# A selective-scan layer with feed-forward: a prologue of its own on six PSUM banks, one table set for Exp and Ln, and twelve units added by VectorE

## What is computed

```python
xz = einsum('bld,ed->ble', hidden, in_proj_w); x, z = xz[..., :1024], xz[..., 1024:]
x = silu(causal_conv4(x, conv_w) + conv_b)
x_dbl = einsum('bld,ed->ble', x, x_proj_w)         # 64 for dt, 16 for B, 16 for C
dt = softplus(einsum(x_dbl[..., :64], dt_proj_w) + dt_proj_b)
A = -exp(A_log)
h = exp(dt * A) * h + dt * x * B                   # per channel and state, over 4096 tokens
y = (sum over n of h * C + x * D) * silu(z)
x1 = layernorm(hidden + einsum(y, out_proj_w))
out = layernorm(x1 + relu(x1 @ Wq1.T + b1) @ Wq2.T + b2)   # Wq: W quantised to -1, 0, 1
```

## Time and profile before

| what | value |
|---|---|
| median of 3 runs | 4861.68 us (4856.44 to 4863.53) |
| profiled execution | 4863.47 us, its span 4861.4 us |
| first scan starts | 91.85 us |
| last scan ends | 3829.8 us |
| busy over the span | PE 92%, DVE 81%, ACT 74%, POOL 66% |

### The profile page before, as it was taken

One profiled execution on the slowest core, in us unless ns is written; L12 is line 12 of the kernel. 1 busy time (PEld: TensorE's weight loads), 2 busy tenths in 40 slices (PEclk: granted clock), 3 DMA queues, 4 the chain that ended last, 5 costly groups with the idle time before them and its releaser, 6 DMA issues.

```text
span 4861.4 us, 85854 instructions
## 1 busy us (share of the span) xinstructions
PE 4458.8 (92%) x23618; PEld 3170.0 (65%) x23618; DVE 3926.1 (81%) x4654; ACT 3613.7 (74%) x6854; POOL 3188.2 (66%) x2471
## 2 busy tenths in 40 slices
PE   6989898989898989989898989898988899999998
PEld 2656565656566666656565656565656588888887
DVE  4989898989898989889898989898989754444444
ACT  4888988889898989898989898989897522222222
POOL 3898978797979888888888888888888300000000
PEclk7999999999999999999999999999999999999999
DMA  2333333333333333323333333333333200000000
GB/s 92 97 104 101 105 103 103 101 103 105 106 100 108 102 106 99 113 92 117 101 109 99 111 94 115 102 105 111 97 131 128 66 27 35 35 35 35 35 35 35
DMA packets 233380, 436.78 MB, mean 90 GB/s; under 512 B 23968, under 2 KB 24096, under 8 KB 232416
## 3 DMA queue, kind: packets, MB, share of 16 engines
q1 hardware_dynamic: 232928, 431.55, 28.0%
HBM read 397.38 MB, written 34.08 MB: 89 GB/s over the span
## 4 chain that ended last, share of the span: by engine, by line
PE 33%; POOL 27%; issue 18%; ACT 13%; DVE 6%; POOLq 1%; DMA 1%; ACTq 0%; DVEq 0%; SPq 0%
POOL dbu L627 22%; PE ht L1365 8%; PE y L1378 5%; PE gemm L1378 5%; ACT ch L688 4%; PE ht L1229 4%; PE gemm L1177 4%; ACT decay L674 3%; PE y L1234 3%; DVE h L933 3%; PE gemm L1213 2%; POOL x L561 2%; POOL carry L601 1%; PE gemm L1204 1%; POOL dtx L574 1%
## 5 line engine op out<-in xcount | busy, mean ns | idle before, releaser
L933 DVE TENSOR_TENSOR_SCAN h<-decay,carry,dbu 128x512 f32<-128x512 f32 x2048 | 2519.7, 1268 | 292.2 <-ACT decay L674 188.8
L627 POOL TENSOR_TENSOR dbu<-dtx,bb 128x1024 f32<-128x1024 f32 x1024 | 2470.3, 2412 | 8.7 <-issue 4.1
L674 ACT ACTIVATE decay<-dt,aneg 128x512 f32<-128x512 f32 x2048 | 1438.9, 705 | 221.6 <-DVE h L933 209.0
L1229 PE MATMUL ht<-ident,h 128*128 128x128 f32 x8192 | 1256.5, 282 | 346.8 <-ACT ch L688 237.7
L1229 PEld LDWEIGHTS ht<-ident,h 128*128 128x128 f32 x8192 | 970.9, 144 | 865.4 <-ACT ch L688 391.5
L688 ACT ACTIVATE ch<-ht,ct 128x256 f32<-128x256 f32 x3456 | 1461.8, 485 | 80.5 <-PE ht L1229 79.4
L1177 PE MATMUL gemm<-xt,win 128*128 128x512 f32 x2048 | 1014.6, 605 | 12.1 <-DMA win<-w_in 7.2
L1234 PEld LDWEIGHTS y<-ident,ch 128*128 128x128 f32 x6912 | 818.4, 144 | 228.0 <-issue 223.2
L1234 PE MATMUL y<-ident,ch 128*128 128x128 f32 x6912 | 923.9, 278 | 0.4 <-ACT ch L688 0.4
L853 ACT ACTIVATE hr<-ht,b1c 128x512 f32<-128x512 f32 x256 | 176.3, 689 | 707.3 <-PE ht L1365 707.3
L601 POOL TENSOR_TENSOR carry<-h,ones_pair 128x2 f32<-128x2 f32 x1022 | 283.7, 278 | 514.2 <-DVE h L933 501.8
(11 more groups left out here) (91 smaller groups left out, 3923.6 us busy)
## 6 DMA issues: line engine op xcount, KB each, us to landing
bb<-b_rows SPq DMA_DIRECT2D x1024, 256.0 KB, 3.5
win<-w_in SPq DMA_DIRECT2D x256, 256.0 KB, 2.6
xt<-x_cm SPq DMA_DIRECT2D x16, 1024.0 KB, 9.3
xres<-x_tm SPq DMA_DIRECT2D x16, 1024.0 KB, 7.6
x<-xres SPq DMA_DIRECT2D x16, 1024.0 KB, 5.2
xr<-x SPq DMA_DIRECT2D x16, 1024.0 KB, 5.4
out<-xr SPq DMA_DIRECT2D x16, 1024.0 KB, 4.3
raw<-w SPq DMA_DIRECT2D x8, 1024.0 KB, 7.6
```

The costliest lines, as they stand in the source:

```text
L627: nc.gpsimd.tensor_tensor(dbu[:, u % 2, :, :], dtx[:, pair(q), :], bb[:, u % BB_RING:u % BB_RING + 1, :].to_broadcast([P, 2, TC]), ALU.mul ...
L674: nc.scalar.activation(DA[j][:, :], dt[:, c.par, i, :], ACT.Exp, scale=aneg[:, i, n:n + 1])\
L933: nc.vector.tensor_tensor_scan(h[:, H_SLOT[u], j, :], DA[j][:, :], dbu[:, u % 2, j, :], carry[:, c.par, n, i:i + 1], ALU.mult, ALU.add).th ...
L1229: ins = nc.tensor.transpose(HT[k][:, tb % 2, j * P:(j + 1) * P], h[:, H_SLOT[u], j, tb * P:(tb + 1) * P], ident[:, :])
```

## The change

- **Prologue.** Chunk 0's products go to six banks (`FIRST_X`: G, HT, Y) and x_proj and the transposes to the two DA banks. xt is loaded in four pieces behind the first block of win; wout is loaded last, on a semaphore of its own, and `conv_in` covers the convolution's two weights alone. The correction of chunk 0 is left out (GpSimd only counts its semaphores up); the silu of a quarter follows the taps of that quarter. Only softplus quarter 0 is done ahead of chunk 0, its excess and its two dtx on VectorE; quarter 1 is done within chunk 0's first units.
- **Tables.** `load_ln_exp` loads the set that has both Exp and Ln, at the start and behind each silu. The four logarithms of a chunk stand singly.
- **Places.** `BY_DVE` has twelve units; all tables of places are set anew.

```diff
-BY_DVE = (2, 3, 9, 17, 38, 39, 45, 47, 52, 58)
+BY_DVE = (1, 3, 9, 12, 17, 38, 39, 45, 47, 54, 57, 60)
-X_GEMM_AT = ((25, 33, 34, 35), (35, 38, 38, 40), (43, 43, 44, 45), (45, 46, 47, 49),
+X_GEMM_AT = ((31, 33, 34, 34), (34, 38, 39, 41), (43, 44, 44, 44), (47, 47, 50, 52),
...
-OUT_AT = ((5, 5, 5, 6, 7, 8, 8, 9),
+OUT_AT = ((2, 2, 4, 6, 7, 9, 9, 10),
...
-EXP_AT = {5: 2, 7: 3, 97: 0, 104: 1}
-LN_AT = {21: (2, 3), 107: (0, 1)}
+EXP_AT = {9: 2, 11: 3, 97: 0, 103: 1}
+LN_AT = {14: (2,), 22: (3,), 106: (0,), 108: (1,)}
-NORM_LN_AT = 107
-NORM_AT = {111: (0, 1), 118: (2, 3)}
+NORM_LN_AT = 105
+NORM_AT = {109: (0,), 110: (1,), 111: (2,), 114: (3,)}
-ADD_AT = {11: 2, 15: 3, 35: 9, 59: 17, 123: 38, 124: 39, 140: 45, 146: 47, 163: 52, 179: 58}
+ADD_AT = {8: 1, 15: 3, 34: 9, 43: 12, 59: 17, 121: 38, 124: 39, 141: 45, 146: 47, 169: 54, 179: 57, 185: 60}
-EXCESS_AT = {12: 2, 13: 3, 55: 0, 58: 1}
-DTX_AT = {3: (2,), 10: (3,), 19: (4,), 20: (5,), 34: (6,), 35: (7,), 56: (0, 1)}
-GATE_AT = {3: (6,), 4: (7,), 60: (0,), 61: (1, 2, 3, 4), 63: (5,)}
-CORR_AT, FIX_AT = 0, 40
+EXCESS_AT = {12: 2, 15: 3, 55: 0, 56: 1}
+DTX_AT = {3: (2,), 9: (3,), 20: (4,), 28: (5,), 29: (6,), 33: (7,), 57: (0,), 59: (1,)}
+GATE_AT = {3: (6,), 4: (7,), 60: (0, 1), 61: (2, 3), 62: (4,), 63: (5,)}
+CORR_AT, FIX_AT = 6, 38
+FIRST_ROUND_AT, FIRST_LN_AT, FIRST_EXCESS_AT, FIRST_SUM_AT = 4, 3, 2, 9
-XT_AT, X_AT, B_AT = 8, 7, 52
+XT_AT, X_AT, B_AT = 16, 1, 56
...
+        FIRST_X = [G[0], G[1], HP[0], HP[1], Y[0], Y[1]]
+        FIRST_XD, FIRST_CT = DA
...
-            load_xt(first, 0)
             load_win(0, "x", 0)
+            for k in range(KM):
+                sp.dma_start(xt[:, 0, k, :], x_cm[k * P:(k + 1) * P, 0:TC]).then_inc(part_in[k] if k + 1 < KM else xt_in, 16)
...
-            pool.wait_ge(weights_in, 16 * N_WEIGHTS)
-            make_corr(first)
-            add_corr(first)
-            for q in (0, 1):
-                excess(first, q)
-            for i in (0, 1):
-                make_dtx(first, i)
+            pool.sem_inc(corr_step, 4)
+            pool.sem_inc(corr_ready, 1)
+            pool.sem_inc(fixed, 1)
...
+            def load_ln_exp():
+                nc.scalar.add_instruction(mybir.InstLoadActFuncSet(name=nc.get_next_instruction_name(),
+                                                                   act_func_set_id=LN_EXP_SET, ins=[], outs=[]))
...
-            for i in range(NB):
-                first_tap(first, i)
-            silu_x(first)
+            first_tap(first, 0)
+            first_tap(first, 1)
+            for q in range(NP):
+                for i in (2 * q + 2, 2 * q + 3):
+                    if i < NB:
+                        first_tap(first, i)
+                wait(act, conv_step, first, TAPS, (2 * q + 2) * (KC - 1))
+                nc.scalar.activation(x[:, 0, pair(q), :], x[:, 0, pair(q), :], ACT.Silu).then_inc(x_ready, 1)
+            load_ln_exp()
             take_xd(first)
+            for i in range(2):
+                take_dt(first, i)
+            softplus_exp(first, 0)
             take_ct(first)
...
+            nc.vector.tensor_tensor(soft[:, 0, :, :], soft[:, 0, :, :], rounded[:, 0, :, :], ALU.subtract)\
+                .then_inc(excess_ready, 1)
+            softplus_sum(first, 0)
+            for i in (0, 1):
+                nc.vector.tensor_tensor(dtx[:, i, :], dt[:, 0, i, :], x[:, 0, i, :], ALU.mult).then_inc(dtx_ready, 1)
```

More of the change, by code:

```diff
@@ L10 @@
 AX = mybir.AxisListType
+LN_EXP_SET = 6
 P = 128
@@ L157 @@
+FIRST_DTX_AT = {max(u, FIRST_SUM_AT // 3 + 1) if i and i[0] in (2, 3) else u: i for u, i in DTX_AT.items()}
+XT_AT, X_AT, B_AT = 16, 1, 56
 LOAD_LAG = 5
@@ L298, in layer @@
         OP = [Y[0], Y[1], G[0], G[1]]
+        conv_in = sem("conv_in")
+        part_in = [sem(f"part_in{k}") for k in range(KM - 1)]
         weights_in = sem("weights_in")
+        wout_in = sem("wout_in")
         alog_in = sem("alog_in")
@@ L632, in chunk @@
                         nc.gpsimd.memset(all_ones[:, :], 1.0).then_inc(ones_set, 1)
+                    if u == FIRST_EXCESS_AT and is_first:
+                        wait(pool, dt_ready, c, NP, 1)
+                        excess(c, 1)
                     if u == CORR_AT and not is_last:
@@ L790, in chunk @@
                         at = 2 * u + k
+                        if is_first and at == FIRST_LN_AT:
+                            softplus_ln(c, 1)
                         if not is_last:
@@ L1032, in between @@
                 def between(at):
+                    if is_first and at == FIRST_ROUND_AT:
+                        softplus_round(c, 1)
+                        softplus_lift(c, 1)
+                    if is_first and at == FIRST_SUM_AT:
+                        softplus_sum(c, 1)
                     if at in ADD_AT:
@@ L1172, in in_proj @@
                     room(kind, chunk, i)
-                    if i == 0:
+                    if i == 0 and not is_first_chunk(chunk):
                         wait(pe, xt_in, chunk, 16, 16)
@@ L1282, in _, with anywhere @@
             first = Chunk(0, 0)
-            room = prologue = rooms([None, None])
+            def anywhere(kind, chunk, i):
+                if kind in ("x", "dt") and i >= len(FIRST_X):
+                    wait_read(pe, kind, chunk, i - len(FIRST_X))
             for i in range(NB):
-                in_proj("x", first, i, range(KM), room, i, NB)
-            pe.wait_ge(weights_in, 16 * N_WEIGHTS)
-            x_proj(first, range(NB), room)
-            transpose_xd(first, room)
-            for i in range(NB):
-                dt_proj(first, i, room)
+                anywhere("x", first, i)
+                wait(pe, win_in[i % 2], first.near(-1), NB * 16, (NB + i // 2 + 1) * 16)
+                for k in range(KM):
+                    if i == 0:
+                        if k + 1 < KM:
+                            pe.wait_ge(part_in[k], 16)
+                        else:
+                            wait(pe, xt_in, first, 16, 16)
+                    ins = nc.tensor.matmul(FIRST_X[i % len(FIRST_X)][:, :], win[:, i % 2, k, :], xt[:, 0, k, :],
+                                           start=(k == 0), stop=(k == KM - 1))
+                ins.then_inc(full["x"], 1)
+            pe.wait_ge(weights_in, 16 * N_WEIGHTS)
+            x_proj(first, range(NB), anywhere)
+            wait_read(pe, "x", first, NB - 1)
+            wait_read(pe, "xd", first, 0)
+            for i in (0, 1):
+                dt_proj(first, i, anywhere)
+            transpose_xd(first, anywhere)
+            for i in range(2, NB):
+                dt_proj(first, i, anywhere)
+            wait_read(pe, "dt", first, len(FIRST_X) - 1)
+            pe.wait_ge(wout_in, 16)
+            prologue = rooms([("dt", first, NB - 2), ("dt", first, NB - 1)])
             def chunk(c, is_first, is_last):
```

144 lines of the change are left out of this document (80 added, 64 removed), and 6 rows, old and new, of the table OUT_AT.

## The result

The changed kernel takes 4739.15 us (median of 4 runs, 4733.51 to 4742.24) against 4862.5; the ratio is 0.9746, 95% interval 0.9731 to 0.9762: 123 us less. The profiled execution took 4733.51 us, its span is 4731.7, 129.7 less than before.

What follows compares the result with a forecast made beforehand. ScalarE was taken to bound units 40 to 63, some 95 us of 233 per chunk. Profiled 4863.5 - 33 (prologue) - 48 (15 periods) = 4782.5; the median lies 1.8 lower, so 4781 us, range 4726 to 4838.

Steps and rivals of the forecast that it cites:

- The prologue: Ahead of the first scan: 36 us less, 3 given back in chunk 0, net -33 us.
- The loads: ScalarE's table loads: four fewer per chunk, 5.1 us of ScalarE; four around the silus stay, 1.28 us each.
- rival E: Table set chosen anew at each Exp, so two loads more per chunk: 4839 us, chance 0.04.
- the drain: ScalarE's table loads: the Trainium skill adds about 1.38 us, 2.66 per switch; the rows do not show it.
- rival C: Whole period: ScalarE's whole relief counts and GpSimd's queueing goes, 6.5 us per chunk: 4731 us, chance 0.16.
- The sum over a period: All stages of a chunk together: -3.2 us per chunk, -48 us over 15 periods.
- units 0 to 3: First stage of a chunk: correction products move behind dbu 6, saving 0.7 us (0 to 1.1).
- Units 4 to 39: Second stage of a chunk: VectorE gets 1.9 us more, TensorE 1.1 less, ScalarE 4.5 less: +0.5 us (-1 to +1.9).
- Units 40 to 51: Third stage of a chunk: keeps its work, change 0.
- Units 52 to 63: Last stage of a chunk: ScalarE gets 4.5 us less, 3.0 taken as gain (bounds 0 and 4.5).
- B: Only the prologue gains; GpSimd takes up ScalarE's relief, period 234.7 us kept: 4829 us, chance 0.20.
- D: Slower: VectorE's extra 3.8 us per chunk come wholly on the path: 4889 us, chance 0.06.

Runs made afterwards that it cites:

- e12: Changed kernel with chunk 0's deferred excess at GpSimd's unit 4 instead of 2 and its sum ahead of unit 6; 4733.9 us, ratio 0.9734.
- e7: Changed kernel without the shared Exp and Ln table set, all load_ln_exp taken out; 4980.2 us, ratio 1.0242.
- e1: Kernel before plus only the table set with Exp and Ln, loaded at the start and behind each silu; 4849.6 us, ratio 0.9974.
- e4: Changed kernel with the ten VectorE units of before and their places (BY_DVE, ADD_AT); 4803.0 us, ratio 0.9876.
- e11: Changed kernel with the old places for TensorE's products, their takes, convolution, skip, residual, statistics, gates, correction and loads; 4803.2 us, ratio 0.9874.
- e10: Changed kernel with the softplus places of before (Exp, Ln, round, lift, sum, excess, dtx); 4778.4 us, ratio 0.9829.
- e5: Kernel before with only the twelve VectorE units and their places (BY_DVE, ADD_AT) of the changed kernel; 4902.2 us, ratio 1.0089.
- e8: Changed kernel with ten VectorE units on new places, 12 and 54 left out; 4754.7 us, ratio 0.9781.
- e9: Changed kernel with the norm's places of before, including its logarithm and VectorE's shift; 4762.4 us, ratio 0.9796.

## Why the prediction was right, and where its size was off

The direction, the order of the parts and the range held; the forecast of 4781 was 42 us too high. Its working gave 81 us where 122 to 130 were found.

**The prologue** came out step by step: TensorE's four rows of 16 without a stop but at the pace of 3.43 us a block, x_proj done by 41.6 (41.3 foreseen), the subtraction 1.23 us (1.2 taken), first scan 56.74 (55.5). The start was 4.37, near the lower bound. The prediction's outer bounds, -25 and -38, do not come out of its terms: with 36 us, a give-back of 0 to 8.5 and 5 more lost they would be -22.5 and -36. The measured -28.7 lies inside both. Mis-sized was what chunk 0 gives back: 3 us taken, 6.4 measured, of which e12 gets 3.9 back; I had added the deferred work, and the price was that GpSimd stood 5.45 us in front of it with the next dbu behind. The bounds of 0 and 8.5 held it; net 28.7 for 33. Chunk 0 took 236.0 us, and "longer than 235" was one of the prediction's own signs of being wrong.

**The loads** went as counted: four per chunk, 1283 ns each, none in the feed-forward part, whose length stayed (1030.3 for 1031.6). The rival E is out. So is the drain that the prediction weighed for rival C: in the traces of before, changed and e7 (165, 65 and 257 loads) ScalarE's next operation stands within 0.02 us behind more than 95 in 100 of the loads.

**The sum over a period** is where it failed: -3.2 taken, -7.05 measured. "ScalarE is the bound of units 40 to 63" and "I take 3.0" for its relief there was the false step. e1 takes 2.57 us off it in that very stage and gets nothing. A busy share of 96% showed that ScalarE had little slack over the stage, not that each of its operations was on the path. In the trace of before the two loads of chunk 4 begin at 1213.70 and 1217.20 us. Ahead of GpSimd's excess the first could give back 0.23 us, since GpSimd is in a dbu until 1215.90; VectorE waits for that excess until 1218.52 and is then held in the shift until 1221.97:

```profile
1212.55 3.35 POOL L627 TENSOR_TENSOR dbu<-dtx,bb 128x1024 f32<-128x1024 f32 x1
1216.13 2.35 POOL L566 TENSOR_TENSOR soft<-soft,rounded 128x1024 f32<-128x1024 f32 x1 [0.23 <-ACT soft L733]
...
1218.52 1.22 DVE L919 SCALAR_TENSOR_TENSOR dt<-soft,dt 128x1024 f32<-128x1024 f32 x1 [0.91 <-POOL soft L566]
```

The long one of the waits for decays (4.6 us in the earlier trace rows) came from the silu of z, five units later.

By stage: units 0 to 3, foreseen -0.7, came to -3.2; with old units (e4), products (e11) or softplus (e10) 2.1, 1.6 and 1.4 of it are lost. The prediction read this stage from chunk 4 alone, where it takes 15.3 us; the even chunks gained 2.1 us, chunks 3, 5 to 13 gained 4.6. Units 4 to 39, +0.5, came to -0.7: the price of 1.9 for VectorE's unit 12 is real (e5 pays 1.7), but retimed products and softplus gave 1.4 and 1.0, and among them unit 12 costs nothing there (122.6 in e8 without units 12 and 54, 122.0 with them). Units 40 to 51, "keep their work: 0", came to -1.5, and all of it is lost with the old product places (e11). Units 52 to 63, -3.0, came to -1.65; the old units (e4) lose 2.3 there, the old norm places (e9) 2.0, the old softplus or product places 0.6 each. VectorE's wait for decays there fell from 7.9 to 6.0 us, where the prediction wanted 4 or less.

So the term that I left out is the new places themselves: I priced moved work at nothing where its cover was there. By the traces they change at least two things: who is issued first where VectorE and GpSimd exclude each other (rounded 1053 to 713 ns over 64, shift 2144 to 154 over 16: 21.8 + 31.8 = 53.6 us of VectorE's time, not all of it on the path, as e10 shows), and what ScalarE has before it when the silus come (e8). What the product places give, as much as the old units cost, stays without a mechanism.

One rival was not tested, TensorE's clock. By the traces it was granted at its lower level for 177 us of chunks 1 to 14 before and 143 changed, 219 in e5 and 284 in e7, most of it around the silus of z: in chunk 4 of before no matmul runs from 1239.9 to 1247.4 us, the clock falls at 1240.7, and a transposing matmul of h then takes 0.42 us for the 0.27 that it took just ahead. The low time is longest where the period is, and these runs don't tell how much of the loss it makes and how much only follows from TensorE's waits. Three us of that stretch (the clock is the number 0.50):

```profile
1241.00:1244.00 3.00, 0.00 (x0) 0.00 (x0) 0.19 (x1) 2.97 (x4) 3.00 (x3) 0.50 0.00 0
```

**The rivals.** C, ScalarE's whole relief, was nearest in time (4731), for a reason that is not borne out: the loads, 5.1 of its 9 us, are worth 0.5 us a period alone (e1), and the units alone cost time (e5). Its other half, dtx and gates spread over more units, was only moved together with other places (e10, e11). B's outcome, a period that the relief leaves as it was, nearly holds for the set alone. D is what the twelve units do by themselves: e5, slower by 0.9%; its price per chunk was 3.8 and 2.7 were measured.

That the forecast of 4781 came within 42 us rests partly on luck: the 3.0 us a chunk taken for ScalarE's relief, of which the loads alone give nothing in that stage (e1), stood in for places priced at nothing.

The undone parts don't add. Against the changed kernel, old units cost 5.0 us per period, norm places 1.9, softplus places 3.1, product places 5.0: 15 us, twice the 7.05 of all together. That the twelve units turn from +2.7 (e5) to -5.0 (e4) per period with what stands around them is shown; which single place turns them is open.

## What to carry to other kernels

A busy share near full in a stage names a candidate, not the path: before pricing relief, look for where inside the stage the other engines' longest single wait ends, and whether the work taken off lies between that and the wait before. A tiny operation whose mean is fourteen times its least duration, as the shift's here, may be held by another engine, and then its place, not its size, sets its time: compare the mean in the lines with the shortest instance in the timeline. Whether the time held is on the path is a second question; the same held shift went with 2.0 us in one kernel and 0.6 in another. In a schedule written out by hand a change of one engine's load and a new set of places have to be judged together: the twelve units alone lost 41 us here, and within the new places they gained.

## What was not expected of the hardware

- VectorE's shift on 128x4 elements took 0.15 us free and 2.3 us when issued behind GpSimd's dbu; the rounding on 128x1024 took 0.67 us free and, begun inside a GpSimd product of 128x512 or 128x1024 in the kernel before, the rest of it plus 0.55, up to 2.22. dbu itself was 2412 ns in the mean before and 2385 after, 2.34 free.
- A table load took 1283 ns in every run, nearly always with 0.02 us or less on either side, also with 14 of them per chunk (e7).
- TensorE's clock (2.4 GHz) fell to 1.2 GHz around the silus of z in every chunk, before and changed; units 52 to 63 held 11.0 and 9.2 us of it in the mean.
